# Attention batches of a fused Flamingo block: six pieces of per-batch work put into other slots

## The reference, cut to what matters

```python
# x: 16 batches x 128 tokens x 256, fp32
x = x + tanh(g_xattn[0]) * wkv(layernorm(x), ctx)           # recurrence over tokens
x = x + tanh(g_ffn[0])   * ternary_ffn(layernorm(x))        # 704 hidden
# third stage: here x[b] is read as 128 channels x 256 positions, 16 heads of 8
q, k, v = Wq @ z + bq, Wk @ ctx + bk, Wv @ ctx + bv         # z = layernorm(x)
dot = mask * (q_h . k_h) / sqrt(8) - (1 - mask) * 1e6
x = x + tanh(g_xattn[1]) * (softmax(dot) * mask) @ v
x = x + tanh(g_ffn[1])   * moe(layernorm(x))                # 8 experts, top 1, plus a shared expert
```

## Time and profile before

| what | value |
|---|---|
| median of 3 runs | 511.44 us (511.41 to 511.58) |
| the profiled execution, its own time | 511.55 us |
| its span, first to last instruction | 509.8 us |
| mean granted TensorE clock | 0.997 of full speed |
| busy over the span | TensorE 93%, VectorE 75%, ScalarE 48%, GpSimd 45% |
| attention's 16 batches with the closing one | about 181 to 377.6 us of the span |
| mixture of experts behind the barrier | its TensorE starts at 377.87 us of the span |

### The profile page before, as it was taken

One profiled execution on the slowest core, in us unless ns is written; L12 is line 12 of the kernel. 1 busy time (PEld: TensorE's weight loads), 2 busy tenths in 40 slices (PEclk: granted clock), 3 DMA queues, 4 the chain that ended last, 5 costly groups with the idle time before them and its releaser, 6 DMA issues. The chain is left out here.

```text
span 509.8 us, 10287 instructions
## 1 busy us (share of the span) xinstructions
PE 474.0 (93%) x3384; PEld 259.0 (51%) x3384; DVE 380.9 (75%) x765; ACT 245.1 (48%) x461; POOL 230.5 (45%) x319
## 2 busy tenths in 40 slices
PE   2999999998999989999999999898999999999993
PEld 2663664754733533333344333333445647788882
DVE  4979889899888779999999999998555624333321
ACT  2751232322232078899999998777512001233331
POOL 3727433155656454867767763213010560042433
PEclk9999999999999999999999999999999999999998
DMA  7750086002675216566666665300022225378843
GB/s 237 213 175 0 16 186 95 2 0 62 181 195 141 66 43 177 148 167 175 165 172 163 179 159 147 82 5 6 1 81 90 74 94 166 120 178 201 193 111 41
DMA packets 67256, 59.96 MB, mean 118 GB/s; under 512 B 10048, under 2 KB 62256, under 8 KB 67216
## 3 DMA queue, kind: packets, MB, share of 16 engines
q1 hardware_dynamic: 63712, 55.24, 39.5%
q0 software_dynamic: 3072, 4.21, 4.9%
q10 hardware_dynamic: 432, 0.00, 0.0%
HBM read 38.90 MB, written 22.50 MB: 120 GB/s over the span
## 5 line engine op out<-in xcount | busy, mean ns | idle before, releaser
L1308 DVE TENSOR_REDUCE MX<-psum 128x2 f32<-128x512 f32 x256 | 162.2, 683 | 9.9 <-PE psum L1173 8.4
L1357 ACT ACTIVATE HP<-psum 128x512 f32<-128x512 f32 x224 | 122.4, 601 | 29.2 <-PE psum L1188 26.8
L1173 PE MATMUL psum<-QKA 60*128 60x256 bf16 x512 | 81.4, 273 | 7.3 <-DVE MX L1308 5.9
L1188 PE MATMUL psum<-QKA 60*128 60x256 bf16 x512 | 81.2, 273 | 1.6 <-DMA QKA<-max_scr 1.1
L1274 PE MATMUL psum<-HP,VP 128*32 128x256 f32 x1024 | 81.8, 391 | 0.3 <-issue 0.2
L588 PE MATMUL psum<-space_a,space_w 128*128 128x512 f32 x160 | 73.1, 601 | 2.8 <-DVE HP L615 2.0
L1173 PEld LDWEIGHTS psum<-QKA 60*128 60x128 bf16 x512 | 31.6, 94 | 64.2 <-DVE MX L1308 43.7
L1945 POOL DMA_INDIRECT out_x<-OE,to_u x16 | 24.9, 1558 | 62.7 <-ACT OE L1980 60.2
L588 PEld LDWEIGHTS psum<-space_a,space_w 128*128 128x128 f32 x160 | 29.0, 190 | 37.4 <-issue 31.9
L2068 PE MATMUL psum<-XT,WE 128*128 128x256 f32 (+1 forms) x192 | 44.0, 379 | 1.0 <-DVE HE L2234 1.0
L199 PE MATMUL psum<-space_a,wsh 128*128 128x512 f32 (+1 forms) x96 | 43.6, 598 | 0.3 <-PEq L1480 0.3
(11 more groups left out here) (203 smaller groups left out, 766.8 us busy)
## 6 DMA issues: line engine op xcount, KB each, us to landing
QKA<-stack_scr SPq DMA_DIRECT2D x32, 480.0 KB, 4.6
stack_scr<-PARTS SPq DMA_DIRECT2D x32, 192.0 KB, 2.1
WE<-in_W SPq DMA_DIRECT2D x16, 352.0 KB
stack_scr<-PARTS SPq DMA_DIRECT2D x32, 128.0 KB, 2.0
XD<-dispatched SPq DMA_DIRECT2D x8, 258.0 KB, 3.8
X<-in_x SPq DMA_DIRECT2D x4, 512.0 KB, 5.7
CTX<-in_ctx SPq DMA_DIRECT2D x4, 512.0 KB, 8.0
MB<-in_mask SPq DMA_DIRECT2D x16, 128.0 KB, 3.2
```

The source lines that it names most:

```text
L1173: return pe.matmul(to[:, tt * T:(tt + 1) * T], QKA[rows, k, 0, h, tt * P:(tt + 1) * P], QKA[rows, k, 1, h, :], start=True, stop=True)
L1188: return pe.matmul(to[:, (m % 2) * T:(m % 2 + 1) * T], QKA[rows, k, 1, h, st * P:(st + 1) * P], QKA[rows, k, 0, h, :], start=True, stop=True)
L1308: dve.tensor_reduce(MX[:, par, head_of(n), :], src[:, :].rearrange("p (a s) -> p a s", a=2), axis=AX.X, op=ALU.max).then_inc(a_red, 1)
L1357: act.activation(PT[:, i % 2, st, 2 * half:2 * half + 2, :].rearrange("p j t -> p (j t)"), TBK3[THIRDS[m]], ACT.Exp).then_inc(a_exp, 1)
```

## The change

Per batch, yT, sums, y, yo and the addition to X each go one slot earlier (TensorE 3 to 2 and 5 to 4; VectorE 3, 4, 5 to 2, 3, 4), and so do the projection of the query on TensorE (6 to 5), its way out of PSUM on ScalarE (7 to 6) and the normalised input on GpSimd (3 to 2, where it now stands ahead of the first subtraction). Part 0 with its subtraction goes one slot later (2 to 3); part 1 stays in slot 4. No instruction is added or removed.

```diff
@@ scalar @@
-                            if p == 7 and there(b, AHEAD_Z):
+                            if p == 6 and there(b, AHEAD_Z):
                                 act_qk(act, b + AHEAD_Z)
-                            if p in (2, 4) and there(b, AHEAD_Q):
-                                act_part(act, b + AHEAD_Q, p // 2 - 1)
+                            if p in (3, 4) and there(b, AHEAD_Q):
+                                act_part(act, b + AHEAD_Q, p - 3)
@@ gpsimd @@
-                            if p in (2, 4) and there(b, AHEAD_Q):
-                                pool_rest(pool, b + AHEAD_Q, p // 2 - 1)
-                            if p == 3 and there(b, AHEAD_Z):
+                            if p == 2 and there(b, AHEAD_Z):
                                 pool_z3(pool, pch, b + AHEAD_Z)
+                            if p in (3, 4) and there(b, AHEAD_Q):
+                                pool_rest(pool, b + AHEAD_Q, p - 3)
@@ tensor @@
-                            if p == 6 and there(b, AHEAD_Z):
+                            if p == 5 and there(b, AHEAD_Z):
...
-                            if p == 3 and there(b, -1):
+                            if p == 2 and there(b, -1):
...
                                 pe_yT(pe, b - 1)
-                            if p == 5 and there(b, -1):
+                            if p == 4 and there(b, -1):
                                 pe_yo(pe, b - 1)
@@ vector @@
+                            if p == 2 and there(b, -1):
+                                dve_sums(dve, ch, b - 1)
                             if p == 3 and there(b, -1):
-                                dve_sums(dve, ch, b - 1)
+                                dve_y(dve, ch, b - 1)
                             if p == 4 and there(b, -1):
-                                dve_y(dve, ch, b - 1)
-                            if p == 5 and there(b, -1):
                                 dve_x3(dve, b - 1)
```

## The result

| | before | changed |
|---|---|---|
| median of 7 runs | 511.44 us | 512.81 us |
| lowest and highest | 511.38 to 511.76 | 512.69 to 514.52 |
| ratio of the times, 95% interval | | 1.0036 [1.0023, 1.0049] |

The change makes the kernel 1.4 us slower, 0.4%.

What follows compares the result with a forecast made beforehand. VectorE was taken to bound the attention block, with 0.89 us of holes per batch. Profiled 511.55 + 2.5 (closing batch) + 0 (loop) = 514.05 us, or 513.9 against the median; range 512.6 to 515.9.

Steps and rivals of the forecast that it cites:

- Closing batch: Last batch: TensorE stands still ahead of yo, waiting for YA behind the hidden piece on VectorE; +2.5 us.
- The upper bound, 2.8: Closing batch: TensorE's idle time ahead of yo if each step waits for the whole of the one before, 2.8 us.
- yT, sums, y, yo and the addition early: Loop: one slot earlier, same order and distances, no VectorE hole in the slots concerned; 0 us.
- Projection: Loop, TensorE slot 6 to 5: gains 0.05 us in each of ten batches, -0.5 us, at best -1.0.
- Copy in slot 6: Loop, ScalarE: query out of PSUM ahead of the last two exponentials costs 0.05 us per batch, +0.5, at worst +2.0.
- Parts: Loop, part 0 to slot 3: ScalarE waits 0.4 us for the subtraction, covered by its later idle time; 0 us.
- The loop: All edits in the steady batches together: 0 us, between -1.0 and +2.0.
- the loop gains what the query's work costs: Rival: loop gains 0.10 us per batch and the copy costs nothing; 512.9 us, chance 0.13.
- faster: Rival: TensorE's lead closes 0.56 us of holes in slots 6 to 0 in ten batches; 508.3 us, chance 0.05.
- the loop loses: Rival: slot 7's exponentials slip 0.2 us, TensorE waits for their bank, holes grow; 515.9 us, chance 0.16.
- The clock: Rival: clock falls to 1.2 GHz behind the closing batch's hole, 3.8 us more; 517.7 us, chance 0.04.

Runs made afterwards that it cites:

- e1: Kernel before, with yT, sums, y, yo and the addition one slot earlier in the closing batch alone: 514.2 us, ratio 1.006.
- e2: Changed kernel, with the closing batch in its old slots, so only the loop is changed: 510.52 us, ratio 0.9979.
- e3: Changed kernel, with the hidden piece of the shared expert again ahead of the sums on VectorE in the closing batch: 511.76 us, ratio 1.0006.
- e9: Kernel before, with only yT and the sums one slot earlier in the loop, closing batch old: 510.42 us, ratio 0.9975.
- e4: Kernel before, with yT, sums, y, yo and the addition one slot earlier in the loop; query's work and closing batch old: 512.5 us, ratio 1.0019.
- e7: Kernel before, with yT, sums, y and yo one slot earlier in the loop; addition, projection, copy, parts and closing batch old: 510.23 us, ratio 0.9977.
- e10: e5 with the query's copy out of PSUM back in slot 7, parts and closing batch old: 509.96 us, ratio 0.9967.
- e8: e2 with the query's copy out of PSUM back in slot 7, behind the last two exponentials: 509.99 us, ratio 0.9966.
- e5: e4 plus the projection in slot 5 and the query's copy out of PSUM in slot 6; parts old: 510.46 us, ratio 0.9979.
- e6: Kernel before, with only part 0 and its subtraction in slot 3 and the normalised input in slot 2: 511.79 us, ratio 1.0006.
- e11: Changed kernel measured again without an edit, on another chip: 514.27 us, ratio 1.0042.
- e12: Changed kernel, with eighteen unused transposes of the identity on TensorE between the last yT and the last yo: 512.8 us, ratio 1.0023.

## Why the prediction was right, and where its terms were off

**Closing batch, +2.5 forecast, +2.45 measured.** Every step of it stands in the rows: the hidden piece between the sums and y, its first half 0.27 behind the sums' start (forecast 0.3), y at 376.06 - 374.52 = 1.54 behind it (forecast 1.6), yo 2.84 behind yT (forecast 2.9). e1 and e2 separate this term from the rest, and e3 splits it. The upper bound, 2.8, was added up wrongly: its own terms give 373.93 + 2.38 + 0.10 - 373.73 = 2.7. Nothing hangs on it.

**yT, sums, y, yo and the addition early, 0 forecast: this step was mis-sized.** "Their order and their distances from each other stay the same" was wrong: what stands directly behind the sums got shorter by 0.06 us. And slots 3 to 5 were said to have no hole of VectorE today, from the one batch of the earlier trace rows; in four of the eight batches of the hardware loop the sums did wait a little for yT. e9 shows that yT and the sums alone bring 1.0 us. The step also treated the five as independent of the query's work. e4 shows that they are not: moved without the projection they lose 1.0 us, 2.3 more than with the addition left in its place (e7). The diff moves both, so that the sum was not hurt, but that was luck, for the reasoning had missed the pair.

**Projection, -0.5 forecast.** e10 is e4 with the projection in slot 5, and the way from 512.5 to 509.96 makes that move worth 2.5 us once the addition has gone. From e9 (510.42) to e10 it is 0.5 for y, yo, addition and projection together. None of this 0.5 is in the hardware loop, where both have a period of 11.48 us; it comes from the written-out batches around it. From L662 to the first sums e9 takes 196.86 - 180.97 = 15.89 us and e10 196.53 - 180.94 = 15.59, and every profile with the early projection is as short there (15.58 or 15.59), while e4 and e7, without it, have 15.89 and 15.90. So 0.3 is the projection's. The rest lies in the last two batches (from the third sums before the barrier to the last ones 372.95 - 347.27 = 25.68 us in e9 and 372.34 - 346.93 = 25.41 in e10), and e7 is as short there as e10, so it belongs to y and yo. The size is near the forecast by luck: the reason that I gave, 0.05 in each of ten batches off the query's work, does not show.

**Copy in slot 6, +0.5 forecast, +0.5 measured,** at 0.05 us per batch, from two pairs of kernels (e2 and e8, e5 and e10). **Parts, 0 forecast:** 0 within the uncertainty of e6, and the wait of ScalarE is 0.30 us where 0.4 was forecast.

**The sum.** Forecast 513.9, measured 512.81, so the kernel lost 1.4 us where 2.5 were forecast, and the time lies near the lower end of the range, 512.6. The loop came to -1.0 instead of 0, and that is nearly all of the difference. The median of e11, 514.27, lies closer to 513.9, but only since the clock's 1.7 us, which the sum had left out, stand in for the gain that it had missed. In time the result is what the rival "the loop gains what the query's work costs" had given, 512.9, but for another reason: the gain sits at the sums, and the batches that have no query work gained 0.06 us each as well. The rival "faster" falls: the holes ahead of the next batch's first scores are still there in every kernel (0.26 and 0.20 in the changed one). The rival "the loop loses" falls with e2.

**The clock** was given a chance of 0.04 and 3.8 us, and both were wrong. It does drop, in some executions and not in others, 7 of 19 going by the mean clock, and it costs 1.7 us, since the clock came back before both pieces were through. With it the changed kernel ends at about 514.3, without it at about 512.8. The Trainium skill, "TensorE: Matmul & The Clock Gate", section "Why this matters for your kernels", warns of idle gaps between bursts of matmuls; the runs agree with that in kind, and show the drop behind a hole of 2.24 us, shorter than the gaps that it warns of. That the hole brings it is shown by the profile of e11, by the 163 runs without the hole, none of them at 0.993 or less, and by e12, which fills it and takes away nothing else. What decides in which execution it happens stays open.

## What to carry to other kernels

A slot that is as good as any other in the steady loop can be a bad one in the closing batch, where other work stands between the steps. Read the order of both engines there first, and keep a filler between two steps of which the second waits for another engine. Two steps on different engines can hang together by their distance in slots (here VectorE's addition and TensorE's projection); then they move together or not at all. Read more than one batch before a wait is put at nothing: here it was in every second one. Here the best version tried takes the loop's new slots, but not those of the closing batch and of the copy (e8 or e10).

## What the runs showed of the hardware that was not expected

- **A reduction right behind the sums can be shorter.** The reciprocal of 128x32 followed by a reduction gives 1.22 us for two reductions in the new slot and 1.28 in the old. In the closing batch the hidden piece's first half takes 0.63 us behind the sums and 0.69 elsewhere. But the kernel before shows 1.22 behind its first sums too, in a written-out batch, so the slot alone doesn't decide it. Why it is so stays open: no run measured the pair by itself.
- **The clock can fall behind a hole of 2.24 us, but not each time:** it did in 7 of the 19 runs of the first result, e1 and e11, going by the mean clock, and in one profile directly. Behind the 1.09 us of e3 one run of twelve has such a mean, and no profile shows it.
- **The entry of a block** (the idle time put down to TensorE's own sequencer at L781) was 1.91 us in the profile of the changed kernel and 0.90 to 0.92 in all the others, at the same instructions. What makes the difference stays open, and so does what lengthened single batches by 0.2 to 0.6 us in the profiles of the changed kernel, of e6 and of e8. In e8 such a batch had a late load of the maxima's parts ahead of it, which was not tried by itself.
